# Attention on one core: lows of q and k formed by VectorE from the bank, exponentials joined for four sums a head group

## The chip, the cores and the metric

One core of one Trainium2 chip runs the whole program in one launch. The metric is the device time of one execution in microseconds (us); the median of several executions stands for a kernel. The engines are TensorE (PE; its weight loads are PEld), VectorE (DVE), ScalarE (ACT), GpSimd (POOL) and SyncE (SP, which issues DMAs).

## The reference

The reference is one transformer block with conditioning, on x of 8 x 1024 x 512, 16 heads of 32, hidden width 2048:

```python
mod = silu(condition) @ Wada + bada
sh_a, sc_a, gt_a, sh_m, sc_m, gt_m = split(mod, 6, axis=1)
xm = layernorm(x, g1, be1) * (1 + sc_a) + sh_a
q, k, v = heads(xm @ Wqkv)
attn = softmax(where(causal, q @ k.T * 32 ** -0.5, -inf))
x = x + gt_a * ((attn @ v) @ Wproj + bproj)
xm = layernorm(x, g2, be2) * (1 + sc_m) + sh_m
x = x + gt_m * (gelu(xm @ W1 + b1) @ W2 + b2)
```

All of it is float32. Products are formed in fp32r, whose operands carry fewer bits, so an operand that needs more is kept as a high (rounded) and a low (what is left), and a product is the sum of three: high by high, high by low, low by high.

## The kernel before

**Stages.** Rows of x are taken in 16 blocks of 512 (`ia`). A block gives 12 items: items 0 to 7 are q and k of a head group (four heads) each, items 8 to 11 are v. The first three blocks are made alone, at the start. Then come 16 bodies (`u`), each with the attention of two head groups; bodies 0 to 12 (`with_a`) also make the items of block `u + 3`, and bodies 0 to 11 (`with_ln`) the layer norm, the turning and the modulation of block `u + 4`. The MLP of 32 blocks of 256 rows follows.

**Steps and slots.** A body has 40 steps, 20 to a head group; I write the steps of the first group as 0 to 19 and of the second as 20 to 39. A step is one chunk of scores: 128 keys by 256 queries (128 in chunks 7, 13, 17 and 19) of four heads. PE forms them in two halves (`scores`, L847, into `psT`), ACT takes the exponentials (`exps`, L1117, into the ring `e`), and two steps make a slot, for which PE forms the products with v one slot later (`values`, L885). Slots 3, 6, 8 and 9 hold chunks on the diagonal; POOL masks these (`mask`, L1675), and `values` waits for the semaphore `masked`.

**Sums of exponentials.** POOL adds the chunks of a slot and of the other slots of its group into a buffer of `es` (`half_add`, L1688, for the first chunk of a slot that isn't the first of its group; `add`, L1705, for the second; `add`, L1712, for the first slot of a group). PE then sums a buffer over the keys with products by ones into `psO`: `added_sums` (L858, 256 queries) for a group that ends in a slot off the diagonal, at steps 9, 15 and 19 (29, 35, 39); `diagonal_sums` (L902 and L907, 128 queries each) for slots 3, 6, 8 and 9. Before the change a group of heads has seven groups of slots (`SUM_GROUPS`): 0 to 2, 3, 4 and 5, 6, 7, 8, 9. Both functions wait for `added`.

**Items in a body.** `A_SHARES` says how many of an item's 12 products (L793 for q and k, L797 for v) stand in each step. An item whose first share is in an odd step starts behind that step's `values` (`late`); the others stand behind the step's scores. All items of a body use one PSUM bank (`psA`, bank 1), so an item waits until the one before is out of it. ACT copies the bank to `qk_hl` (`a_copy`, L1107, the full value in the place of the low); DVE makes the high from it (`a_high`, L1363, a maximum of the copy with itself that rounds); POOL subtracts (`a_low`, L1666); SP stores both. `formed` sets the lags of these steps. PE waits for `a_copied` alone. The turned rows of the next block (`a_turn`, L765, steps 23, 29, 33 and 35) use the same bank.

**VectorE's own order.** Maxima of scores are reduced from `psS` (`max_item`, L1375 adds the mask, L1379 reduces) at steps 1, 3, 5, 7, 9, 11, 15, 17 and 19 of each group; PE forms the next piece only when `psS` is read. `max_join` (L1386) stands at step 12, statistics (L1314) at 8, 10, 12 and 14, the aggregate and `veps` (L1321, L1323) at 15, `normalise` (L1330) at 17 to 20. POOL makes `rstd` (L1659) at step 15 and waits for `veps`.

Of the kernel before, what the change touches and what calls it, by code (L numbers as in the profile page):

```python
# [5 lines left out]
ALU = mybir.AluOpType  # L6
# [3 lines left out]
F32R = mybir.dt.float32r  # L10
# [14 lines left out]
SLOTS = NCH // 2  # L25
# [8 lines left out]
AHEAD = 3  # L34
A_TURNS = 4

A_NQK, A_NV = 8, 4
A_ITEMS = A_NQK + A_NV
A_MM = 12
A_SHARES = ((6, 0, 6), (2, 8, 2), (6, 0, 6), (1, 5, 1, 5), (2, 8, 2), (5, 1, 5, 1)) * 2  # L40
A_STORE_LAG = 2

LATE_END, HIGH_LATE, LOW_LATE, STORE_LATE = 5, 2, 3, 4


Q, K = 0, 1
HIGH = (1, 0)
LOW = (0, 1)
QK_RING = 4
V_RING = 4  # L50

TURN_AT, TURN_AFTER = (23, 29, 33, 35), (7, 9, 10, 11)
# [95 lines left out]
DIAG_SLOTS = [i for i in range(SLOTS) if 2 * i in DIAG]  # L148
OTHER_SLOTS = [i for i in range(SLOTS) if i not in DIAG_SLOTS]

SUM_GROUPS = {True: [(0, 1, 2), (3,), (4, 5)] + [(i,) for i in range(6, SLOTS)], False: [(i,) for i in range(SLOTS)]}

HALF_ADDED = [i for g in SUM_GROUPS[True] for i in g[1:]]
HALF_ADDS = len(HALF_ADDED)
# [45 lines left out]
def build(nc, x, cond, Wqkv, Wproj, bproj, W1, b1, W2, b2, g1, be1, g2, be2, Wada, bada, out):  # L200
# [26 lines left out]
    with ExitStack() as keep:  # L227
        sems = {}

        def sem(name):  # L230
            if name not in sems:
                sems[name] = keep.enter_context(nc.semaphore(name))
            return sems[name]
# [116 lines left out]
        A_NLO = A_NQK  # L350
# [58 lines left out]
        def item_bank(n, alone):  # L409

            return n % 2 if alone and n <= TURN_AFTER_ALONE[0] else 1
# [13 lines left out]
        def _(sp):  # L425
# [30 lines left out]

            def a_store(ia, n):

                sp.wait_ge(sem("a_lo_done"), ia * A_NLO + n + 1)
                past(sp, "sp")  # L460
                sp.dma_start(qk_dram[n % 2, n // 2, :, :, bass.ds(ia * XB, XB)],
                             qk_hl[:, n % QK_RING]).then_inc(qk_stored[n % QK_RING], 16)
# [252 lines left out]
        def _(pe):  # L715
# [35 lines left out]
            def a_turn(ia, k, alone):  # L751

                bank = turn_bank(ia, k, alone)
                if k == 0:
                    pe.wait_ge(sem("xn_ready"), ia + 1)
                if not alone:
                    pe.wait_ge(sem("a_copied"), (ia - 1) * A_ITEMS + TURN_AFTER[k])
                elif ia > 0 and k == 0:
                    pe.wait_ge(sem("a_copied"), (ia - 1) * A_ITEMS + TURN_AFTER_ALONE[0])
                elif ia > 0:  # L760
                    pe.wait_ge(sem("a_modulated"), ia * A_TURNS + k)
                elif k >= 2:
                    pe.wait_ge(sem("a_modulated"), k - 1)
                for r in range(NXR):
                    mm = pe.transpose(psA[:, bank, r * P:(r + 1) * P], normalised(ia)[:, r, k * P:(k + 1) * P], ident[:])  # L765
                mm.then_inc(sem("a_turned"), 1)

            def a_item(ia, n, first, end, alone, turns):


                bank = item_bank(n, alone)
                if first == 0:
                    if alone and ia == 0 and n < 2:
                        pe.wait_ge(sem("a_modulated"), A_TURNS - 1 + n)
                    elif alone and n == 0:
                        pe.wait_ge(sem("a_modulated"), ia * A_TURNS + A_TURNS)
                    elif alone and n == 1:
                        pe.wait_ge(sem("a_copied"), ia * A_ITEMS)
                    elif alone and n <= TURN_AFTER_ALONE[0]:
                        pe.wait_ge(sem("a_copied"), ia * A_ITEMS + n - 1)  # L780
                    elif turns and n in TURN_AFTER:
                        pe.wait_ge(sem("a_modulated"), (ia + 1) * A_TURNS + TURN_AFTER.index(n) + 1)
                    else:
                        pe.wait_ge(sem("a_copied"), ia * A_ITEMS + n)
                for q in range(first, end):
                    k = q // 3
                    if n == 0 and q % 3 == 0:
                        pe.wait_ge(sem("xm_lo"), ia * KT + k + 1)
                    ends = dict(start=(q == 0), stop=(q == A_MM - 1), skip_group_check=True)
                    if n < A_NQK:  # L790
                        m = n % 2 * IPB + n // 2
                        a, w = ((xm_h, wqkv_h), (xm_l, wqkv_h), (xm_h, wqkv_l))[q % 3]
                        mm = pe.matmul(psA[:, bank, :], w[:, k, m * P:(m + 1) * P], a[:, k, :], **ends)  # L793
                    else:
                        m = n - A_NQK
                        a, w = ((xm_h, wqkv_h), (xm_h, wqkv_l), (xm_l, wqkv_h))[q % 3]
                        mm = pe.matmul(psA[:, bank, :], a[:, k, m * P:(m + 1) * P], w[:, k, 2 * D:3 * D], **ends)  # L797
                    if n == A_ITEMS - 1 and q % 3 == 2 and k < KT - 1:
                        mm.then_inc(sem("xm_freed"), 1)
                if end == A_MM and first < A_MM:  # L800
                    mm.then_inc(sem("a_formed"), 1)
# [268 lines left out]
        def _(act):  # L1070
# [26 lines left out]
            def a_copy(ia, n, alone):  # L1097

                if n < A_NQK:
                    wait(act, qk_stored[n % QK_RING], (ia * (A_NQK // QK_RING) + n // QK_RING) * 16)  # L1100
                    dst, src = qk_hl[:, n % QK_RING, LOW[n % 2]], psA[:, item_bank(n, alone), :]
                else:
                    m = n - A_NQK
                    wait(act, v_stored[m % V_RING], (ia * (A_NV // V_RING) + m // V_RING) * 16)
                    dst, src = vout[:, m % V_RING], psA[:, item_bank(n, alone), :]
                act.wait_ge(sem("a_formed"), ia * A_ITEMS + n + 1)
                act.activation(dst, src, ACT.Copy).then_inc(sem("a_copied"), 1)  # L1107
# [167 lines left out]
        def _(dve):  # L1275
# [79 lines left out]
                dve.wait_ge(sem("xm_hi"), ia * KT + k + 1)  # L1355
                dve.tensor_tensor(low, modulated(ia, k), high.bitcast(F32), ALU.subtract).then_inc(sem("xm_lo"), 1)

            def a_high(ia, n):

                if n < A_NQK:  # L1360
                    dve.wait_ge(sem("a_copied"), ia * A_ITEMS + n + 1)
                    full = qk_hl[:, n % QK_RING, LOW[n % 2]]
                    dve.tensor_tensor(qk_hl[:, n % QK_RING, HIGH[n % 2]].bitcast(F32R), full, full, ALU.max)\  # L1363
                       .then_inc(sem("qk_hi"), 1)

            def max_item(u, ahead, n, masks):

# [27 lines left out]
            def body(u, with_a, with_ln, after_a):  # L1395
                last = isinstance(u, int) and u == NU - 1
                for s in range(BODY_STEPS):
                    h, r = divmod(s, NCH)
                    if r == JOIN_AT and not (last and h == 1):
                        max_join(u, h + 1)  # L1400
                    if r == MAX_TURN_AT and not (last and h == 1):
                        max_row(u, h + 1)
                    if with_a and s == SPLIT_LAST_AT and not (isinstance(u, int) and u == 0):
                        a_split(u + AHEAD, KT - 1)
                    if with_ln and s in SPLIT_AT:
                        a_split(u + AHEAD + 1, SPLIT_AT[s])
                    if r in MAX_AT:
                        d, n = MAX_AT[r]
                        if not (last and h + d >= 2):
                            max_item(u, h + d, n, with_a)  # L1410
                    item = formed(u, s, 1, HIGH_LATE, with_a, after_a)
                    if item:
                        a_high(*item)
                    if with_ln and s in LN_STATS_AT:
                        ln_stats(u + AHEAD + 1, LN_STATS_AT.index(s))
                    if with_ln and s == LN_AGGR_AT:
                        ln_aggregate(u + AHEAD + 1)
                    if with_ln and s in LN_NORM_AT:
                        normalise(u + AHEAD + 1, LN_NORM_AT.index(s))
# [215 lines left out]
        def _(pool):  # L1635
# [89 lines left out]
            def body(u, with_a, with_ln, after_a, pieces):  # L1725
                for s in range(BODY_STEPS):
                    mask(u, s)
                    if s % 2 == 0:
                        half_add(u, s // 2, with_a)
                    else:  # L1730
                        add(u, s // 2, with_a)
                    item = formed(u, s, 1, LOW_LATE, with_a, after_a)
                    if item:
                        a_low(*item)
                    if with_ln and s == LN_AGGR_AT:
                        a_rstd(u + AHEAD + 1)
                    if isinstance(u, int) and u == NU - 1 and s == FIRST_RSTD_AT:
                        rstd_2(0)
                    for part in range(2):
                        q = PIECE_AT.get(s - PIECE_LOW_LAG - 2 * part)  # L1740
                        if q is not None and q < pieces:
                            piece_low(u, q, part)
# [76 lines left out]
```

## Time and profile before

| what | value |
|---|---|
| median of 3 executions | 3148.65 us (3148.61 to 3149.07) |
| the profiled execution | 3149.18 us, span 3147.5 us |
| granted TensorE clock, mean of the span | 0.999 |
| busy: PE, DVE, POOL, ACT | 98%, 78%, 54%, 45% |
| chain that ended last: PE, DVE | 90%, 5% |
| stage of items alone | 0 to about 149 us |
| 16 bodies | about 149 to 1547 us |
| MLP | about 1547 us to the end |

Busy shares are means over stages with different limits. A PE row's end is modelled, so consecutive PE rows overlap: what a group of products costs is read from its start to the start of the next group.

### The profile page before, as it was taken

The numbers are of one execution on the slowest core, as the hardware profiler recorded it, in microseconds if no ns is written. First come the engines' busy times: TensorE is split into PE (matmuls) and PEld (weight loads), VectorE is DVE, ScalarE is ACT, GpSimd is POOL, SyncE is SP. The second block draws the span as 40 slices with busy tenths as digits, with TensorE's granted clock in tenths as the row PEclk, the third lists the DMA queues.
The fourth block names the chain that finished last, engine by engine and source line by source line (L and its number), as shares of the span: only waits on it lengthen the run. The fifth ranks groups of instructions, "written<-read, shape, count | busy, mean of one in ns | idle before, by whom it ended". The sixth has DMA issues, their size and how long they took to land.

```text
span 3147.5 us, 64741 instructions
## 1 busy us (share of the span) xinstructions
PE 3099.2 (98%) x22888; PEld 2417.4 (77%) x22888; DVE 2451.6 (78%) x2975; ACT 1429.7 (45%) x2876; POOL 1704.9 (54%) x1385
## 2 busy tenths in 40 slices
PE   8999999999999999999899999999999999999999
PEld 5677777777777777766688888888888888888888
DVE  5688887787888778766787878878787787878874
ACT  4355555555555555566543333333333333333333
POOL 3388888888888888888742323232322322323232
PEclk9999999999999999999999999999999999999999
DMA  7666566666656666676713222221222313222120
GB/s 251 211 191 193 170 193 183 177 188 184 194 174 187 183 177 187 181 192 178 180 41 81 57 63 68 52 80 46 74 57 63 79 41 80 57 63 67 53 67 14
DMA packets 304625, 391.81 MB, mean 124 GB/s; under 512 B 24296, under 2 KB 206088, under 8 KB 304448
## 3 DMA queue, kind: packets, MB, share of 16 engines
q1 hardware_dynamic: 292336, 371.86, 41.7%
q10 hardware_dynamic: 12112, 17.42, 1.6%
q8 instruction: 132, 2.16, 0.3%
q14 instruction: 45, 0.37, 0.0%
HBM read 270.66 MB, written 118.00 MB: 123 GB/s over the span
## 4 chain that ended last, share of the span: by engine, by line
PE 90%; DVE 5%; issue 2%; DMA 1%; ACT 1%; POOL 1%; SPq 0%; DVEq 0%; ACTq 0%; POOLq 0%
PE psY L1025 22%; PE psH L1013 14%; PE psA L793 9%; PE psT L847 9%; PE psH L1016 7%; PE psA L885 7%; PE psA L797 6%; PE psP L922 6%; PE psS L816 4%; DVE mx L1379 2%; PE psA L858 2%; PE psA L765 1%; DVE psS L1375 1%; PE psA L907 1%; PE psA L902 1%
## 5 line engine op out<-in xcount | busy, mean ns | idle before, releaser
L1654 POOL TENSOR_TENSOR h_l<-h_full,h_h 128x256 fp32r<-128x256 f32 x512 | 451.2, 881 | 1099.5 <-ACT h_h L1255 1099.5
L1117 ACT ACTIVATE e<-psT 128x512 f32<-128x512 f32 (+1 forms) x1202 | 605.6, 555 | 377.0 <-PE psT L847 373.6
L1379 DVE TENSOR_REDUCE mx<-psS 128x4 f32<-128x2048 f32 (+3 forms) x384 | 665.9, 1755 | 118.6 <-PE psS L816 80.5
L1252 ACT ACTIVATE h_full<-h_full,b1c 128x256 f32<-128x256 f32 x512 | 260.4, 509 | 995.1 <-DVE h_full L1555 995.1
L1013 PE MATMUL psH<-a_l,w1p_h 128*128 128x512 f32 x2048 | 547.7, 389 | 1.0 <-ACT o_sb L1125 0.8
L1555 DVE TENSOR_REDUCE h_full<-psH 128x256 f32<-128x512 f32 x512 | 346.8, 677 | 238.8 <-PE psH L1016 230.6
L1712 POOL TENSOR_TENSOR es<-e 128x512 f32<-128x512 f32 (+1 forms) x242 | 444.9, 1839 | 159.5 <-ACT e L1117 75.6
L1013 PEld LDWEIGHTS psH<-a_l,w1p_h 128*128 128x128 f32 x2048 | 384.1, 188 | 83.1 <-ACT o_sb L1125 1.0
L847 PEld LDWEIGHTS psT<-qst,kst 97*128 97x128 f32 x2404 | 349.1, 189 | 113.7 <-issue 70.2
L847 PE MATMUL psT<-qst,kst 97*128 97x256 f32 (+1 forms) x2404 | 410.4, 290 | 3.4 <-ACT e L1117 1.7
L1025 PE MATMUL psY<-w_h,h_h 128*128 128x512 f32 x1024 | 404.2, 395 | 0.8 <-POOL h_l L1654 0.8
L1025 PE MATMUL psY<-w_l,h_h 128*128 128x512 f32 x1024 | 403.9, 394 | 0.0
L1025 PE MATMUL psY<-w_h,h_l 128*128 128x512 f32 x1024 | 398.4, 389 | 0.0
L1016 PEld LDWEIGHTS psH<-a_l,w1p_l 128*128 128x128 f32 x2048 | 313.1, 189 | 39.9
L1016 PE MATMUL psH<-a_l,w1p_l 128*128 128x256 f32 x2048 | 325.4, 282 | 0.0
L885 PE MATMUL psA<-e,vst 128*32 128x256 f32 (+1 forms) x5120 | 313.3, 362 | 0.3 <-POOL e L1675 0.2
L885 PEld LDWEIGHTS psA<-e,vst 128*32 128x32 f32 x5120 | 144.0, 109 | 114.0 <-issue 34.9
L1531 DVE STREAM_TRANSPOSE a_full<-xc 32x256 f32<-32x256 f32 x512 | 223.4, 436 | 9.4
L1467 DVE RECIPROCAL sums_in<-sums_in 128x256 f32<-128x256 f32 x128 | 222.7, 1743 | 7.9 <-DMA sums_in<-sums 7.8
L1666 POOL TENSOR_TENSOR qk_hl<-qk_hl 128x512 fp32r<-128x512 f32 x128 | 166.9, 1306 | 112.9 <-ACT qk_hl L1210 64.6
L1025 PEld LDWEIGHTS psY<-w_h,h_l 128*128 128x128 f32 x1024 | 192.5, 188 | 43.6
L1255 ACT ACTIVATE h_h<-h_full 128x256 fp32r<-128x256 f32 x512 | 214.2, 418 | 16.3
(118 smaller groups left out, 4927.5 us busy)
## 6 DMA issues: line engine op xcount, KB each, us to landing
qk_split<-qk_hl SPq DMA_DIRECT2D x128, 512.0 KB, 3.6
kst<-qk_split SPq DMA_DIRECT2D x128, 256.0 KB, 3.9
qst<-qk_split SPq DMA_DIRECT2D x128, 256.0 KB, 4.1
xin<-in_x_dram SPq DMA_DIRECT2D x64, 256.0 KB, 3.6
values<-vout ACTq DMA_DIRECT2D x64, 256.0 KB, 2.4
kmx<-qk_split SPq DMA_DIRECT2D x32, 512.0 KB, 4.7
qmx<-qk_split SPq DMA_DIRECT2D x32, 512.0 KB, 5.8
kst<-qk_split SPq DMA_DIRECT2D x128, 128.0 KB, 3.9
```

The costliest lines, as they stand in the source:

```text
L793: mm = pe.matmul(psA[:, bank, :], w[:, k, m * P:(m + 1) * P], a[:, k, :], **ends)
L847: mm = pe.matmul(bank[:, d, 0:w], kst[0:97, hd, key_cols(kt, h)], qst[0:97, q0 // HALF, hd, q0 % HALF:q0 % HALF + w], start=True, stop=Tru ...
L885: mm = pe.matmul(psO[HD * hd:HD * (hd + 1), c:c + w], vst[:, h, kt, HD * hd:HD * (hd + 1)], e[:, (2 * t + d) % ERING, hd, 0:w], start=(kt ...
L1013: pe.matmul(psH[:, m % 4].rearrange("p (s r) -> p s r", s=2), w1_h[:, k, cols], a_hl[par][:, :, k, :], start=(k == 0), stop=(k == KT - 1), ...
L1016: mm = pe.matmul(psH[:, m % 4, 0:RA], w1_l[:, k, cols], a_h[par][:, k, :], start=False, stop=(k == KT - 1), skip_group_check=True)
L1025: mm = pe.matmul(psY[:, r, :], a[:, m % 4, r * P:(r + 1) * P], w[:, w2_at(m), :], start=(m == 0 and n == 0), stop=(m == FT - 1 and n == 2) ...
L1117: act.activation(e[:, s % ERING, 2 * hp:2 * hp + 2, 0:w], score_bank(s, hp, with_a)[:, :, 0:w], ACT.Exp, scale=SCALE).then_inc(sem("exp_do ...
L1252: act.activation(h_full[:, m % 4, :], h_full[:, m % 4, :], ACT.Gelu, bias=b1c[:, m:m + 1])\
L1379: reduce = dve.tensor_reduce(mx[:, part, :, qt], psS[:, :, col:col + w], AX_X, ALU.max)
L1555: dve.tensor_reduce(h_full[:, m % 4, :], psH[:, m % 4].rearrange("p (s r) -> p r s", s=2), AX_X, ALU.add)\
L1654: return pool.tensor_tensor(dst, full, high.bitcast(F32), ALU.subtract)
L1712: pool.tensor_tensor(to, first, second, ALU.add).then_inc(sem("added"), 1)
```

## The change

In the bodies (the stage alone is as it was) ACT's copy of a q or k item is rounded to fp32r on its way out and goes to the place of the high. DVE's `a_low` subtracts that high from the full value in the PSUM bank and writes the low; `a_high` of DVE and `a_low` of POOL are gone there. The bank is free for the next item, or for the first turn, when `a_low` has read it, so PE and SP now wait for its semaphore `a_lo_body`. `a_low` stands one step behind the end of the item, ahead of that step's `max_item`, where `a_high` stood behind it. `SUM_GROUPS` has four groups: 0 to 3, 4 to 6, 7 and 8, 9. `A_SHARES` gives shares of (4, 8, 0) where (2, 8, 2) stood, and (6, 0, 6, 0) for (5, 1, 5, 1).

```diff
-A_SHARES = ((6, 0, 6), (2, 8, 2), (6, 0, 6), (1, 5, 1, 5), (2, 8, 2), (5, 1, 5, 1)) * 2
+A_SHARES = ((6, 0, 6), (4, 8, 0), (6, 0, 6), (1, 5, 1, 5), (4, 8, 0), (6, 0, 6, 0)) * 2
-LATE_END, HIGH_LATE, LOW_LATE, STORE_LATE = 5, 2, 3, 4
+LATE_END, STORE_LATE = 5, 4
-SUM_GROUPS = {True: [(0, 1, 2), (3,), (4, 5)] + [(i,) for i in range(6, SLOTS)], False: [(i,) for i in range(SLOTS)]}
+SUM_GROUPS = {True: [(0, 1, 2, 3), (4, 5, 6), (7, 8), (9,)], False: [(i,) for i in range(SLOTS)]}
@@ a_store (SP)
-                sp.wait_ge(sem("a_lo_done"), ia * A_NLO + n + 1)
+                if isinstance(ia, int) and ia < AHEAD:
+                    sp.wait_ge(sem("a_lo_done"), ia * A_NLO + n + 1)
+                else:
+                    sp.wait_ge(sem("a_lo_body"), (ia - AHEAD) * A_NLO + n + 1)
@@ a_turn (PE)
-                if not alone:
+                if not alone and TURN_AFTER[k] <= A_NQK:
+                    pe.wait_ge(sem("a_lo_body"), (ia - 1 - AHEAD) * A_NLO + TURN_AFTER[k])
+                elif not alone:
@@ a_item (PE)
+                    elif not alone and 0 < n <= A_NQK:
+                        pe.wait_ge(sem("a_lo_body"), (ia - AHEAD) * A_NLO + n)
@@ a_copy (ACT)
+                    if not alone:
+                        dst = qk_hl[:, n % QK_RING, HIGH[n % 2]].bitcast(F32R)
@@ DVE
-            def a_high(ia, n):
+            def a_low(ia, n):
...
-                    full = qk_hl[:, n % QK_RING, LOW[n % 2]]
-                    dve.tensor_tensor(qk_hl[:, n % QK_RING, HIGH[n % 2]].bitcast(F32R), full, full, ALU.max)\
-                       .then_inc(sem("qk_hi"), 1)
+                    dve.tensor_tensor(qk_hl[:, n % QK_RING, LOW[n % 2]].bitcast(F32R), psA[:, item_bank(n, False), :],
+                                      qk_hl[:, n % QK_RING, HIGH[n % 2]], ALU.subtract).then_inc(sem("a_lo_body"), 1)
@@ body (DVE), ahead of max_item
+                    item = ended(u, s - 1, with_a, after_a)
+                    if item:
+                        a_low(*item)
@@ body (DVE), behind max_item
-                    item = formed(u, s, 1, HIGH_LATE, with_a, after_a)
-                    if item:
-                        a_high(*item)
@@ body (POOL)
-                    item = formed(u, s, 1, LOW_LATE, with_a, after_a)
-                    if item:
-                        a_low(*item)
```

Three places show how the change moves instructions. The first is POOL at steps 15 to 19 of a body with layer norm, before (`e` are exponentials, `es` their sums, `qk_hl` an item):

```order
L1712 TENSOR_TENSOR es<-e 128x1024
L1659 TENSOR_TENSOR rstd<-veps,power 128x4
L1675 AFFINE_SELECT e<-e 128x4x128
L1666 TENSOR_TENSOR qk_hl<-qk_hl 128x512
L1675 AFFINE_SELECT e<-e 128x4x128
L1712 TENSOR_TENSOR es<-e 128x4x128
```

and with the change:

```order
L1720 TENSOR_TENSOR es<-e 128x1024
L1667 TENSOR_TENSOR rstd<-veps,power 128x4
L1683 AFFINE_SELECT e<-e 128x4x128
L1696 TENSOR_TENSOR es<-es,e 128x1024
L1683 AFFINE_SELECT e<-e 128x4x128
L1713 TENSOR_TENSOR es<-es,e 128x4x128
```

Between the two masks of slot 8 an add of 1024 elements a partition stands in the place of the item's subtraction of 512.

The second is DVE at steps 11 to 15 of such a body, before:

```order
L1379 TENSOR_REDUCE mx<-psS 128x4
L1386 TENSOR_TENSOR mxc<-mx 128x32
L1314 BN_STATS stats<-xin 128x6
L1363 TENSOR_TENSOR qk_hl<-qk_hl 128x512
L1393 CAST m_row<-psS 32x128
```

and with the change:

```order
L1387 TENSOR_REDUCE mx<-psS 128x4
L1394 TENSOR_TENSOR mxc<-mx 128x32
L1323 BN_STATS stats<-xin 128x6
L1371 TENSOR_TENSOR qk_hl<-psA,qk_hl 128x512
L1401 CAST m_row<-psS 32x128
```

The order is the same; the fourth row, which nobody but POOL waited for, is now the one that frees the bank for item 4, at step 13.

The third is PE at step 19, before:

```order
L847 MATMUL psT<-qst,kst 128x128 x4
L793 MATMUL psA<-xm_h,wqkv_l 128x512
L816 MATMUL psS<-kmx,qmx 128x512 x4
L858 MATMUL psA<-es,ones 32x256 x4
L885 MATMUL psA<-e,vst 32x256 x4
L885 MATMUL psA<-e,vst 32x128 x4
L902 MATMUL psA<-e,ones 32x128 x4
L907 MATMUL psA<-es,ones 32x128 x4
```

and with the change:

```order
L854 MATMUL psT<-qst,kst 128x128 x4
L823 MATMUL psS<-kmx,qmx 128x512 x4
L892 MATMUL psA<-e,vst 32x256 x4
L892 MATMUL psA<-e,vst 32x128 x4
L914 MATMUL psA<-es,ones 32x256 x4
```

The sums of a slot off the diagonal (L858) are gone, those of slot 8 are one quad of 256 queries that wait for both adds, and the item's single product has moved to step 18.

## Rows read from the trace of the kernel before

**Rows 1.** The page, section 1: busy time and share of each engine.

```profile
PE 3099.2 (98%) x22888; PEld 2417.4 (77%) x22888; DVE 2451.6 (78%) x2975; ACT 1429.7 (45%) x2876; POOL 1704.9 (54%) x1385
```

**Rows 2.** Windows of 100 us: length, then busy PE, PEld, DVE, ACT, POOL.

```profile
700.00:800.00 100.00, 99.39 (x1007) 71.23 (x1006) 82.15 (x75) 57.52 (x114) 82.28 (x54) 1.00 0.63 184
```

**Rows 3.** Timeline, PEld: step 3 in two consecutive bodies (start, duration).

```profile
705.21 0.30 PEld L816 LDWEIGHTS psS<-kmx,qmx 32*128 32x128 f32 x8 [0.20 <-DVE mx L1379]
...
797.27 0.30 PEld L816 LDWEIGHTS psS<-kmx,qmx 32*128 32x128 f32 x8 [0.20 <-DVE mx L1379]
```

**Rows 4.** Timeline, PE at step 9: sums, values, diagonal sums, then item 3.

```profile
718.90 0.64 PE L858 MATMUL psA<-es,ones 128*32 128x256 f32 x8
...
719.36 0.83 PE L885 MATMUL psA<-e,vst 128*32 128x256 f32 x16
...
720.01 0.40 PE L902 MATMUL psA<-e,ones 128*32 128x128 f32 x8
...
720.23 0.40 PE L907 MATMUL psA<-es,ones 128*32 128x128 f32 x8
...
720.56 0.50 PE L793 MATMUL psA<-xm_h,wqkv_h 128*128 128x512 f32 x1
```

**Rows 5.** Groups by form, 300 to 1500 us: POOL's full add (busy, mean ns).

```profile
L1688 POOL TENSOR_TENSOR es<-es,e 128x1024 f32<-128x1024 f32 x67 | 159.8, 2385 | 5.8 <-ACT e L1117 3.5
```

**Rows 6.** By source line, DVE: duration in ns, min/median/max, first and last start.

```profile
L1363 DVE TENSOR_TENSOR qk_hl<-qk_hl x104: 676/1016/2511, 156.6 to 1315.1; 128x512 fp32r<-128x512 f32 x104
L1375 DVE TENSOR_TENSOR psS<-psS,mask_q x135: 698/1217/1233, 92.2 to 1316.6; 128x1024 f32<-128x1024 f32 x81, 128x512 f32<-128x512 f32 x54
L1323 DVE TENSOR_SCALAR veps<-aggr x16: 169/1617/1636, 14.5 to 1196.2; 128x4 f32<-128x4 f32 x16
```

**Rows 7.** Timeline, steps 11 to 13: POOL, DVE, ACT's copy of item 3, PE's item 4.

```profile
725.42 2.39 POOL L1688 TENSOR_TENSOR es<-es,e 128x1024 f32<-128x1024 f32 x1
726.93 0.93 DVE L1386 TENSOR_TENSOR mxc<-mx 128x32 f32<-128x32 f32 x1
727.00 0.60 ACT L1107 ACTIVATE qk_hl<-psA 128x512 f32<-128x512 f32 x1 [0.29 <-PE psA L793]
727.78 0.68 DVE L1314 BATCH_NORM_STATS2 stats<-xin 128x6 f32<-128x512 f32 x1
728.23 0.50 PE L793 MATMUL psA<-xm_h,wqkv_h 128*128 128x512 f32 x1
728.39 2.44 DVE L1363 TENSOR_TENSOR qk_hl<-qk_hl 128x512 fp32r<-128x512 f32 x1
```

**Rows 8.** Timeline, steps 15 to 19: exponentials of step 15, POOL, `veps`, PE's sums.

```profile
732.14 0.59 ACT L1117 ACTIVATE e<-psT 128x512 f32<-128x512 f32 x1
734.65 2.39 POOL L1712 TENSOR_TENSOR es<-e 128x1024 f32<-128x1024 f32 x1
735.43 1.63 DVE L1323 TENSOR_SCALAR veps<-aggr 128x4 f32<-128x4 f32 x1
737.14 1.39 POOL L1659 TENSOR_TENSOR rstd<-veps,power 128x4 f32<-128x4 f32 x1
738.51 0.63 POOL L1675 TENSOR_SCALAR_AFFINE_SELECT e<-e 128x512 f32<-128x512 f32 x1
739.11 1.29 POOL L1666 TENSOR_TENSOR qk_hl<-qk_hl 128x512 fp32r<-128x512 f32 x1
741.43 1.28 POOL L1712 TENSOR_TENSOR es<-e 128x512 f32<-128x512 f32 x1 [0.26 <-POOL e L1675]
742.86 0.43 PE L907 MATMUL psA<-es,ones 128*32 128x128 f32 x8
```

**Rows 9.** Timeline, step 23: ACT's copy of item 6, PE's maxima, PE's first turn.

```profile
749.67 0.60 ACT L1107 ACTIVATE qk_hl<-psA 128x512 f32<-128x512 f32 x1 [0.44 <-PE psA L793]
750.04 0.51 PE L816 MATMUL psS<-kmx,qmx 32*128 32x256 f32 x8
750.48 0.66 PE L765 MATMUL psA<-ident,xin 128*128 128x128 f32 x4
```

## The prediction

> **What bounds the kernel now.** The page comes first: PE is busy for 98% of the span, no other engine for more than 78% [rows 1]. The change touches only the 13 bodies that make items, so I read the windows of that stage next: PE 99.4 us of 100, POOL and DVE 82.3 and 82.2 each [rows 2]. So PE's own work sets the time there, but two engines follow at four fifths, and both share the step order with PE. The same step of two consecutive bodies lies 92.06 us apart [rows 3]: that is my unit, and every term below is counted per body. The timeline of one body then tells what stands near PE's waits. Twelve bodies have the layer norm; one has not.
>
> **What it takes from PE.** Three sums of slots off the diagonal go in each head group. One costs 719.36 - 718.90 = 0.46 us, from its start to that of `values` [rows 4]. Six a body: -2.76 us. The joined slots 3, 6 and 8 had two quads of 128 queries, 0.22 us to the next start and 0.33 to the item's [rows 4]; now they have one quad of 256, which at the price of L858 is 0.46 and some 0.1 of the change to the next tile. 0.55 against 0.56: nothing. The number of items' products is the same; fewer and larger shares I set at 0. If all else stayed hidden, 26 head groups would give 26 x 3 x 0.46 = 36 us.
>
> **What it moves to and from POOL.** Eight subtractions of 1.29 us [rows 8] leave a body, and six full adds of 2.39 us come [rows 5]: +4.0 us, so 82 becomes about 89% of a body that PE would run in 89.3 us. On average that still fits. Locally it doesn't, see (b).
>
> **What it puts on PE's path.** Before, an item waited for ACT's copy alone. Now it waits for copy, then DVE. DVE's new subtraction isn't in this trace. Its bounds: the instruction that it replaces, two operands from SBUF, took 676 to 2511 ns, median 1016; the mask's add, one operand from a bank and one from SBUF, took 698 at 512 elements, and 1217 to at most 1233 at 1024, so without spread [rows 6]. I take 0.70, the row with the same kinds of operands, and keep 1.02 and 2.51 as the far end. A DVE instruction of 32 elements ended just when POOL's add did (see a). The Trainium skill (SBUF — State Buffer, "SBUF: two separate sides") has a rule that fits it: a DVE instruction with two SBUF inputs and a GpSimd instruction that reads SBUF shut each other out for the whole instruction. By it the 0.70 holds, since one input comes from a bank, and the sum is the one below; but the rule also speaks against the change, since more full adds on GpSimd hold the join and its like more often. Now the places, each against the timeline:
>
> (a) *Step 13, item 4.* PE starts it at 728.23 in the trace; the copy of item 3 ended at 727.60. DVE was then in the join (0.93 us for 32 elements, to 727.86, while POOL's add ended at 727.81) and in the statistics; it began `a_high` at 728.39, which held up nobody on PE [rows 7]. In the changed kernel PE gets there about 0.35 us earlier, 727.87: 0.46 gained at step 9, 0.1 lost there on `added`. DVE ends the reduction of step 11 at about 726.0, 0.9 earlier (no `a_high` ahead of it). But POOL's half add of slot 5, at 725.42 in the trace behind two subtractions [rows 7], now starts with its exponentials at about 722.5, the second add runs from 724.9 to 727.3 and holds the join till then. Join 727.3, statistics (0.60 to the next start) 727.9, low 728.6. PE waits 728.6 - 727.87 = 0.75 us.
>
> (b) *Steps 15 to 20, POOL.* In the trace PE waited for POOL's add of slot 8 already: it ended at 742.71, the sums began at 742.86, 0.29 later than the quad before them allows [rows 8, 4]. In the changed kernel the exponentials of step 15 end at about 733.8 instead of 732.73 (two products more in step 13, the wait of (a), and ACT's copy of item 4 now ahead of them). POOL: add of slot 7 from 733.97 to 736.35; `veps` isn't held by it any more and takes 0.17 [rows 6], so `rstd` runs from 736.6 to 738.0; mask 0.63, dependence 0.26, full add 2.38 in the place of the subtraction of 1.28, mask up to 0.8, 0.26, add 1.28: end at 743.55. PE's own way would reach these sums at about 742.0. With 0.15 of latency it goes on at 743.7, where before it did at 742.86, and then forms 256 queries. I make it a wait of 1.6 us more than before, and the first head group ends 1.0 us *later* than before although three of its sums are gone.
>
> (c) *Step 23, the first turn.* It begins 0.81 us after the start of the copy of item 6, right behind the maxima [rows 9]. Now copy (0.60), low (0.70) and two semaphores of 0.05 to 0.1 must end first: 1.43 us. PE waits 0.6.
>
> (d) Small ones at steps 7, 9 and 27 (the low ahead of the mask's add moves a reduction by up to 0.4) and less waiting at 11: +0.15 together. In the second head group POOL's slot 8 ends just as PE comes; nothing more there.
>
> **The sum.** A body with the norm: -2.76 + 0.75 + 1.6 + 0.6 + 0.15 = +0.3 us; twelve give +4. The body without norm has no `rstd` and no statistics: (a) falls to 0.2, (b) to 0.4, (c) is absent, so -2.0. Together +2 us on 3149.18 of the profiled execution, which lies 0.5 above the median of the runs: 3150.7, say 3151 us. So the forecast is no change that a measurement could tell; it tells about 0.2%, 6.3 us, from none. Its own range: each of the three waits may be off by 0.3 us a body, 12 x 0.5 = 6 us: 3144 to 3157.
>
> **Rivals.**
> *The waits don't form.* If POOL's add doesn't hold the join in (a), the low ends before 727.9, the exponentials of step 15 come 0.75 earlier and all of (b) with them: 12 x 0.75 = 9 us less, 3142. If the masked and joined adds of (b) also end in time, 12 x 2.35 = 28 us less: 3123; without any wait 3113. For it: the stalls of POOL on L858 go too, and DVE sheds 8 x (1.02 - 0.70) us a body at the medians. Against it: (b) follows from durations that hardly vary, and (c) is latency alone.
> *Slower: the low is locked out by POOL.* If DVE's subtraction behaves as the instruction that it replaces, 1.02 us at the median, both (a) and (c) grow by 0.32, and a full block of 1.8 us is possible at either. Two blocks of half that size are 2 x 0.9 x 12 = 22 us, the median 2 x 0.32 x 12 = 8: 3159 to 3173. It decides from a mean of 0.95 us on. Against it: the mask's add doesn't vary.
> *Slower: POOL becomes the bound in the second group as well.* Its slot 8 ends with no margin; 0.5 us there are 6 us, and delays carry over to the next body: 3157 to 3163.
> *The change doesn't do what it says.* The order shows that it does; no case of its own.
>
> **How the numbers follow.** Forecast (waits eat the gain) 0.44. The waits mostly don't form: 0.31. Slower by the low 0.13, by POOL 0.12, of which 0.01 lies within 0.2%. Cut at 6.3 us: faster 0.31, same 0.45, slower 0.24. The range reaches down to 3126, where (a) and most of (b) are gone, and up to 3163; what is left out is the case of next to no wait, 0.1, and that of a low blocked at its worst, 0.1.
>
> **What would show it.** Right: rows of L892 and L914 that start about 1 us late at step 19 and name POOL; a turn (L772) at step 23 and item 4 at step 13 that name DVE's low, L1371; a low of 0.70 without spread; a body of 92.3 us. Wrong: a body of 90 to 91 us with no such waits (the first rival), a spread of L1371 up to 2.5 us (the second), PE waits for POOL at step 39 (the third).

## The result, and the profile after

Median of 6 executions: 3161.52 us (3160.38 to 3162.35), against 3148.77 (3148.28 to 3149.07, 6 executions) for the kernel before, run in turn on the same chip. The ratio is 1.0040, with a 95% interval of 1.0028 to 1.0052. The change makes the kernel 12.7 us slower. That lies in the range (3126 to 3163), but the forecast was no change, 3151 us and at most 3157 by its own bounds, and the measurement tells 12.7 us from none.

The page, section 1, of the changed kernel [as rows 1], and the window of 100 us in the stage of the bodies [as rows 2]; the last three numbers of the window's row are the granted clock, the DMA share and GB/s:

```profile
PE 3069.3 (97%) x21640; PEld 2392.1 (76%) x21640; DVE 2418.3 (77%) x2975; ACT 1430.5 (45%) x2876; POOL 1747.8 (55%) x1359
```

```profile
700.00:800.00 100.00, 95.27 (x883) 67.53 (x872) 79.29 (x73) 56.19 (x111) 86.32 (x54) 1.00 0.63 184
```

PE has 1248 matmuls less and is busy 30 us less, and yet the span grew from 3147.5 to 3159.9: in the window it is idle for 4.7 us of 100, where before it was 0.6. POOL went from 82.3 to 86.3. Step 3 of two consecutive bodies [as rows 3]:

```profile
806.31 0.30 PEld L823 LDWEIGHTS psS<-kmx,qmx 32*128 32x128 f32 x8 [0.48 <-DVE mx L1387]
...
899.58 0.30 PEld L823 LDWEIGHTS psS<-kmx,qmx 32*128 32x128 f32 x8 [0.49 <-DVE mx L1387]
```

The period is 93.27 us, 1.21 more than before. From step 3 of body 0 to step 3 of body 12 the twelve bodies with the layer norm took 14.3 us more; the body without it took 85.28 us for 87.11, 1.8 less. The spans differ by 12.4. The timeline of PE in one body shows all its new waits (the bracket is the idle time and its releaser):

```profile
829.73 0.50 PE L800 MATMUL psA<-xm_h,wqkv_h 128*128 128x512 f32 x1 [0.76 <-DVE qk_hl L1371]
...
842.75 0.86 PE L892 MATMUL psA<-e,vst 128*32 128x256 f32 x16 [0.51 <-POOL e L1683]
...
844.19 0.64 PE L914 MATMUL psA<-es,ones 128*32 128x256 f32 x8 [0.58 <-POOL es L1713]
...
852.69 0.63 PE L770 MATMUL psA<-ident,xin 128*128 128x128 f32 x4 [0.59 <-DVE qk_hl L1371]
...
891.56 0.64 PE L914 MATMUL psA<-es,ones 128*32 128x256 f32 x8 [0.65 <-POOL es L1713]
...
894.99 0.56 PE L823 MATMUL psS<-kmx,qmx 32*128 32x128 f32 x8 [0.27 <-DVE mx L1387]
...
899.58 0.51 PE L823 MATMUL psS<-kmx,qmx 32*128 32x256 f32 x8 [0.28 <-DVE mx L1387]
```

In order: step 13 (a), step 19 twice (b), step 23 (c), and then three that the prediction's sum did not have: step 39, and steps 1 and 3 of the next body. A wait of 0.35 for ACT's `vout` at step 33 is left out; it was there before, as long and as often (4.2 us in 12). The same summed over the execution (total us, times, longest):

```profile
PE psA L914 <- POOL es L1713: 14.6, 24, 0.7
PE psS L823 <- DVE mx L1387: 11.0, 34, 1.2
PE psA L800 <- DVE qk_hl L1371: 9.5, 13, 0.9
PE psA L770 <- DVE qk_hl L1371: 7.2, 12, 0.6
...
PE psA L892 <- POOL e L1683: 6.4, 13, 0.5
```

Of these only L823 had a counterpart before, with 5.2 us in 16 waits. The new subtraction, by source line [as rows 6], in ns:

```profile
L1371 DVE TENSOR_TENSOR qk_hl<-psA,qk_hl x104: 660/691/693, 152.7 to 1322.0; 128x512 fp32r<-128x512 f32 x104
```

It hardly varies, where the instruction that it replaces went up to 2511.

What happens around step 39, DVE and POOL:

```profile
885.26 1.15 POOL L1683 TENSOR_SCALAR_AFFINE_SELECT e<-e 128x512 f32<-128x512 f32 x1 [0.57 <-ACT e L1126]
...
886.57 2.40 POOL L1696 TENSOR_TENSOR es<-es,e 128x1024 f32<-128x1024 f32 x1 [0.16 <-POOL e L1683]
...
888.49 0.76 DVE L1363 CAST xm_h<-xin 128x512 fp32r<-128x512 f32 x1
...
888.92 0.82 POOL L1683 TENSOR_SCALAR_AFFINE_SELECT e<-e 128x512 f32<-128x512 f32 x1
...
889.91 1.51 POOL L1713 TENSOR_TENSOR es<-es,e 128x512 f32<-128x512 f32 x1 [0.16 <-POOL e L1683]
890.21 1.49 DVE L1363 CAST xm_h<-xin 128x512 fp32r<-128x512 f32 x1
...
892.65 2.28 DVE L1387 TENSOR_REDUCE mx<-psS 128x4 f32<-128x2048 f32 x1
```

POOL's last add of slot 8 ends at 891.42; PE stood idle from 890.91 to 891.56. In the trace of before the same place had room:

```profile
783.83 1.77 POOL L1675 TENSOR_SCALAR_AFFINE_SELECT e<-e 128x512 f32<-128x512 f32 x2 [1.11 <-ACT e L1117]
785.86 1.28 POOL L1712 TENSOR_TENSOR es<-e 128x512 f32<-128x512 f32 x1 [0.26 <-POOL e L1675]
...
790.11 0.40 PE L907 MATMUL psA<-es,ones 128*32 128x128 f32 x8
```

There the add ended at 787.14, 2.97 us before PE came. POOL's chain from the first mask to the last add has grown from 3.31 us to 6.16, and PE would come 5.65 us after that mask's start where it came 6.28: so POOL is 0.51 late, and PE goes on 0.14 after it.

While these masks and adds run, DVE's splits of the next block take longer: a cast 0.76 and 1.49, where in the trace of before the two took 0.42 and 0.86. The reduction of step 39 starts 3.0 us after the start of its products (889.62), before 1.7; PE's maxima at step 1 wait for it, and those of step 3 for the next.

### The profile page after: what moved, and what is told of

It reads as the page before. It is cut to its first block, busy times and chain, and to the rows that moved or that the text cites. A ratio compares the mean times of both kernels' runs of the same rounds, so it can differ in the third digit from the quotient of the medians.

```text
span 3159.9 us, 62131 instructions
## 1 busy us (share of the span) xinstructions
PE 3069.3 (97%) x21640; PEld 2392.1 (76%) x21640; DVE 2418.3 (77%) x2975; ACT 1430.5 (45%) x2876; POOL 1747.8 (55%) x1359
## 4 chain that ended last, share of the span: by engine, by line
PE 80%; DVE 9%; issue 5%; POOL 2%; ACT 2%; DMA 1%; ACTq 0%; DVEq 0%; SPq 0%; POOLq 0%
PE psY L1032 22%; PE psH L1020 14%; PE psA L800 8%; PE psH L1023 7%; PE psT L854 6%; PE psP L929 6%; PE psA L892 5%; PE psA L804 5%; DVE mx L1387 5%; PE psS L823 3%; PE psA L770 1%; DVE psS L1383 1%; DVE xm_h L1363 1%; POOL es L1720 1%; PE psA L914 1%
## 5 line engine op out<-in xcount | busy, mean ns | idle before, releaser
L1720 POOL TENSOR_TENSOR es<-e 128x1024 f32<-128x1024 f32 (+1 forms) x164 | 338.8, 2067 | 142.7 <-ACT e L1126 128.9
L1696 POOL TENSOR_TENSOR es<-es,e 128x1024 f32<-128x1024 f32 x156 | 372.1, 2385 | 43.6 <-ACT e L1126 29.0
L892 PE MATMUL psA<-e,vst 128*32 128x256 f32 (+1 forms) x5120 | 314.8, 363 | 6.4 <-POOL e L1683 6.4
L1713 POOL TENSOR_TENSOR es<-es,e 128x1024 f32<-128x1024 f32 x156 | 289.4, 1855 | 20.2 <-POOL e L1683 10.8
L892 PEld LDWEIGHTS psA<-e,vst 128*32 128x32 f32 x5120 | 136.9, 109 | 123.8 <-issue 58.6
```

The source lines that it names most:

```text
L892: mm = pe.matmul(psO[HD * hd:HD * (hd + 1), c:c + w], vst[:, h, kt, HD * hd:HD * (hd + 1)], e[:, (2 * t + d) % ERING, hd, 0:w], start=(kt ...
L1696: pool.tensor_tensor(es[:, place], es[:, place], e[:, 2 * t % ERING], ALU.add)\
L1713: pool.tensor_tensor(to, to, second, ALU.add).then_inc(sem("added"), 1)
L1720: pool.tensor_tensor(to, first, second, ALU.add).then_inc(sem("added"), 1)
```

## The experiments

Eleven kernels ran, in three batches, each in turn with the kernel before (3149.5, 3149.1 and 3148.7 us); the third batch, of the last three kernels, on another chip than the first two. The question of the first four: which of the three parts costs what, and are they separate? The period is that of the turn's rows in the timeline (L770, or L765 before), around 300 to 650 us.

| kernel | median us | ratio, 95% interval | period us |
|---|---|---|---|
| before | 3149 | | 92.08 |
| the change | 3161.5 | 1.0028 to 1.0052 | 93.27 |
| shares alone | 3189.3 | 1.0108 to 1.0141 | |
| four sums alone | 3268.3 | 1.0356 to 1.0390 | |
| low from the bank alone | 3287.4 | 1.0411 to 1.0446 | |
| low and shares, seven sums | 3160.7 | 1.0023 to 1.0048 | 93.01 |
| the change, join at 13 | 3153.7 | 1.0005 to 1.0025 | 92.60 |
| low, shares, join at 13, seven sums | 3152.8 | 1.0002 to 1.0022 | 92.34 |
| the change, five sums | 3140.5 | 0.9965 to 0.9985 | 91.31 |
| **five sums, join at 13** | **3133.3** | 0.9932 to 0.9968 | 90.66 |
| before, with five sums | 3232.2 | 1.0240 to 1.0274 | |
| six sums, join at 13 | 3146.5 | 0.9983 to 1.0002 | 91.57 |
| five sums, join at 13, turn behind values | 3132.2 | 0.9927 to 0.9960 | 90.44 |

### Shares alone

Kernel before, with

```diff
-A_SHARES = ((6, 0, 6), (2, 8, 2), (6, 0, 6), (1, 5, 1, 5), (2, 8, 2), (5, 1, 5, 1)) * 2
+A_SHARES = ((6, 0, 6), (4, 8, 0), (6, 0, 6), (1, 5, 1, 5), (4, 8, 0), (6, 0, 6, 0)) * 2
```

> Only the shares of the items' products are changed (4, 8, 0 and 6, 0, 6, 0); q's and k's lows and the sums are as before. My theory (the loss comes from waits for the low, for joined sums and for VectorE behind GpSimd) gives no work and no wait here: within 3 us of before, body 92.1 +- 0.2 us. The rival that the shares themselves cost, because the exponentials of steps 5, 15 and 24 start two products (0.45 us) later: 0.3 us or more a body, 3152 to 3158.

3189.3 us: the expectation was wrong. An item that ends a step earlier brings DVE's maximum for its high a step forward, to where POOL's two adds of a joined slot run. Timeline of this run, POOL and DVE at steps 7 to 9, and PE's maxima at 9:

```profile
733.28 2.38 POOL L1705 TENSOR_TENSOR es<-es,e 128x1024 f32<-128x1024 f32 x1
...
733.55 2.66 DVE L1363 TENSOR_TENSOR qk_hl<-qk_hl 128x512 fp32r<-128x512 f32 x1
736.13 0.69 DVE L1375 TENSOR_TENSOR psS<-psS,mask_q 128x512 f32<-128x512 f32 x1
...
739.20 0.56 PE L816 MATMUL psS<-kmx,qmx 32*128 32x128 f32 x8 [1.22 <-DVE mx L1379]
```

The 0.7 us instruction takes 2.66, the mask's add and the reduction behind it are late, and PE waits 1.22 for `psS`. Over the execution these waits make nearly all of the 39.8 us lost, since before they came to 5.2:

```profile
PE psS L816 <- DVE mx L1379: 44.3, 43, 1.5
```

So the spread of rows 6, which cost nothing before, was a matter of place.

### Four sums alone

```diff
-SUM_GROUPS = {True: [(0, 1, 2), (3,), (4, 5)] + [(i,) for i in range(6, SLOTS)], ...
+SUM_GROUPS = {True: [(0, 1, 2, 3), (4, 5, 6), (7, 8), (9,)], ...
```

> Only the sums are joined; GpSimd keeps its subtractions. TensorE has 2.8 us a body less to do, GpSimd 14.3 us more (75.7 + 14.3 = 90.0 busy). Theory: GpSimd in its order becomes the bound of the body, with 1 to 3 us of dependences on top: body 91 to 94 us, 3140 to 3175, PE's waits name GpSimd's adds at slots 3, 6 and 8. Rival (GpSimd hides it): body 89.3 us, 3113.

3268.3, far above the expected. POOL, with its eight subtractions kept, is busy 815 us of the 900 from 200 to 1100, and PE waits for it:

```profile
PE psA L885 <- POOL e L1675: 64.0, 48, 2.9
PE psA L907 <- POOL es L1705: 33.8, 64, 0.6
```

98 us of waits less 36 us of sums taken from PE would be 62, and it came to 119: most of the rest went with PE's clock, by the estimate of the last section. The sum of waits for `psS` also went up, from 5.2 to 10.5 us.

### Low from the bank alone

The whole change but `A_SHARES` and `SUM_GROUPS`.

> Only the low is moved to VectorE; shares and sums are as before. Theory: item 4 at step 13 and the first turn at step 23 wait for the low, 0.5 to 0.8 and 0.6 us a body with the norm, and the 0.3 us wait for GpSimd at step 19 goes: +0.8 to +1.1 a body, 3158 to 3163; no PE wait on GpSimd. Rival (the low is harmless and the loss is all in the joined sums): 3146 to 3150.

3287.4, again far above. With the old shares an item that ends in step 5, 15, 19 or 25 leaves the next one, a step on, waiting for a low that stands behind a reduction on DVE. PE at step 16 of this run, and the waits summed (with 7.2 us of the turn's, as in the change, 103 in all):

```profile
708.67 0.49 PE L800 MATMUL psA<-xm_h,wqkv_h 128*128 128x512 f32 x1 [1.50 <-DVE qk_hl L1371]
```

```profile
PE psA L800 <- DVE qk_hl L1371: 68.6, 51, 2.1
PE psA L804 <- DVE qk_hl L1371: 26.9, 13, 2.1
```

So each of the three parts by itself makes the kernel slower, by 40, 119 and 138 us, and together they cost 13. The new shares are there for the low, and the low on DVE for the sums. None of the three can be priced alone.

### Low and shares, with the seven groups of before

> The changed kernel with the sums of before (low on VectorE, new shares). Theory: as with the low alone plus little from the shares, 3157 to 3165, so that the joined sums give in all about nothing (their 33 us of products go into waits for GpSimd and VectorE). Rival (the joined sums are what costs): 3148, 13 below the changed kernel.

3160.7, as expected. Its waits are two, and both are of those that the prediction priced:

```profile
PE psA L800 <- DVE qk_hl L1371: 8.9, 12, 0.9
PE psA L770 <- DVE qk_hl L1371: 7.1, 12, 0.6
```

0.74 and 0.6 us a body: (a) and (c). The waits of steps 19, 39, 1 and 3 aren't there. So the joined sums, which take 2.76 us a body from PE, bring those waits with them, and of the 2.76 us nothing is left: the body is 93.01 us without the joins and 93.27 with them.

### The join of the maxima behind the low (step 13)

```diff
-                    if r == JOIN_AT and not (last and h == 1):
-                        max_join(u, h + 1)
...
                     item = ended(u, s - 1, with_a, after_a)
                     if item:
                         a_low(*item)
+                    if r == JOIN_AT + 1 and not (last and h == 1):
+                        max_join(u, h + 1)
```

with the third statistics at step 13 as well (`LN_STATS_AT` 8, 10, 13, 14).

> The changed kernel, with VectorE's join of the maxima and the third statistics moved from step 12 to step 13, behind the low of item 3 (the step 12 ahead of the low is then empty). Theory (the join, held by GpSimd's add, keeps the low late, and by it the exponentials of step 15 and GpSimd's chain): PE's wait at step 13 for L1371 (0.76 us, 12 times) goes, and GpSimd's end at step 19 comes up to 0.7 us earlier: 0.8 to 1.4 us a body, 3145 to 3152 us. Rival (the join only moves to where the maxima's turn at step 14 waits for it): PE waits for L1394 at step 14 and the time stays at 3158 to 3164. Second rival (GpSimd's adds alone set step 19): only the 0.76 goes, or less, 3152 to 3158.

3153.7: 7.8 us of the change's 12.7 are gone (the theory's sum, 10 to 17, was too high; its second rival's figure fits). DVE around step 13 in this run:

```profile
545.56 0.69 DVE L1371 TENSOR_TENSOR qk_hl<-psA,qk_hl 128x512 fp32r<-128x512 f32 x1 [1.20 <-ACT qk_hl L1116]
546.17 0.18 DVE L1394 TENSOR_TENSOR mxc<-mx 128x32 f32<-128x32 f32 x1
```

The wait for L1371 at L800 (9.5 us) is no longer in the list. But the two rows of waits for POOL (L914 and L892) are word for word those of the change. So (a) and (b) are two causes. When the exponentials of step 15 come earlier, POOL's chain and PE come to step 19 earlier alike: POOL's last add of slot 8 ends 37.07 us after the products of step 3, where in the change it is 37.73.

> The same move of the join, with the seven groups of sums of the kernel before (so: lows from the bank, new shares, old sums). The run with these sums and without the move gave 3160.72 and had two waits on PE, 12 times each: 0.74 us for the low at step 13, 0.6 for the turn at step 23. Theory: the first goes, 9 us, 3150 to 3153. Rival: the wait moves to the maxima's turn, 3158 to 3162.

3152.8, as expected: with the seven sums the same move gives 8.0 us (93.01 to 92.34 a body).

### Slots 7 and 8 as groups of their own

```diff
-SUM_GROUPS = {True: [(0, 1, 2, 3), (4, 5, 6), (7, 8), (9,)], ...
+SUM_GROUPS = {True: [(0, 1, 2, 3), (4, 5, 6), (7,), (8,), (9,)], ...
```

> The changed kernel, but slots 7 and 8 are groups of their own again (five groups of sums). It gives back one sum of 0.46 us a head group, 0.92 a body, 12 us in all, and GpSimd's full add of 2.38 us between the masks of slot 8 is gone. Theory (POOL's slot 8 costs more than the sum it saves): the waits at steps 19 (0.51 + 0.58) and 39 (0.65) go, 1.7 us a body, and with them the waits for maxima at steps 1 and 3 if these come from the same lateness (0.55): net gain 0.8 to 1.4 us a body, 3145 to 3152. Rival (the waits only uncover something else of the same lateness, such as the exponentials): 3160 to 3170.

3140.5, 8.6 below the kernel before, and better than expected. PE has two sums a body more to form, 0.92 us, and yet the body becomes 1.96 us *shorter*. The rows of the waits for the low (9.5 and 7.2 us) are those of the change; what else is left of its waits:

```profile
PE psS L823 <- DVE mx L1387: 4.4, 10, 1.2
```

Both POOL lines are gone, and L823 went from 11.0 us in 34 waits to 4.4 in 10. At step 39 DVE is back to what it did before the change:

```profile
874.75 0.86 DVE L1363 CAST xm_h<-xin 128x512 fp32r<-128x512 f32 x1
...
876.25 2.29 DVE L1387 TENSOR_REDUCE mx<-psS 128x4 f32<-128x2048 f32 x1
```

The reduction starts 1.4 us after its products (874.81) instead of 3.0. That settles steps 1 and 3: they hung on POOL's work of slot 8 at step 39, by way of DVE's splits. The join of 7 and 8 thus cost 0.92 + 1.96 = 2.9 us a body for 0.92 gained. The waits that the trace names are 0.51 + 0.58 + 0.65 + 0.27 + 0.28 = 2.3 of it; 0.6 isn't named by any row.

> Both: the join moved to step 13, and slots 7 and 8 apart. If the two causes are separate, the gains add up: 3136 to 3144 us, below the kernel before (3148.8), with the turn's wait of 0.6 us at step 23 left. If they are one (the low of step 13 is what makes GpSimd late at step 19): the same as the better of the two, 3145 to 3152.

3133.3 us, ratio 0.995 (0.9932 to 0.9968): the two gains add (93.27 - 0.67 - 1.96 = 90.64, measured 90.66), the time is a little below the 3136 to 3144 expected, and this version beats both kernels. PE is busy 98.85 of 100 us in the window of 700 to 800, POOL 83.91. One wait of the change is left, the turn's, with the row that it had (L770, 7.2 us in 12 waits).

### What the low is for, and what slot 6 is worth

Kernel before with the five groups:

> The kernel before (full copy, high on VectorE, low on GpSimd, its shares) with the five groups of sums of the run before this one: 0 to 3, 4 to 6, 7, 8, 9. Theory (the lows on GpSimd leave no room for joined slots 3 and 6; only with them gone do these joins pay): PE waits for GpSimd (L1675, L1705) at slots 3 and 6, 1.5 us each as in the run with four groups (3268), but not at slot 8: 3190 to 3235 us. Rival (the five groups pay whoever forms the lows, and four groups failed by slots 7 and 8 alone): 3149 - 24 = 3125 to 3135 us.

3232.2, as the theory said. POOL and PE at slot 6 of this run:

```profile
756.26 2.37 POOL L1705 TENSOR_TENSOR es<-es,e 128x1024 f32<-128x1024 f32 x1
...
758.59 0.64 POOL L1675 TENSOR_SCALAR_AFFINE_SELECT e<-e 128x512 f32<-128x512 f32 x1
...
759.39 2.38 POOL L1688 TENSOR_TENSOR es<-es,e 128x1024 f32<-128x1024 f32 x1 [0.16 <-POOL e L1675]
...
761.72 1.09 POOL L1675 TENSOR_SCALAR_AFFINE_SELECT e<-e 128x512 f32<-128x512 f32 x1
...
762.96 0.86 PE L885 MATMUL psA<-e,vst 128*32 128x256 f32 x16 [1.49 <-POOL e L1675]
```

An item's subtraction at 752.55 (1.29 us) stands ahead of the adds of slot 5, and from there POOL has next to no gap up to slot 6's second mask, for which `values` wait 1.49 us. With the lows on DVE the same five groups bring no wait for POOL at all. So the move of the low earned nothing by itself (with seven sums and the join at 13, where it costs least, the kernel takes 3152.8 against 3149.1); it made room for the joins of slots 3 and 6. This run has the old shares as well. The new ones go with the low on DVE, and what they would do here with the low on POOL was not run.

Five groups and the join at 13, but slot 6 alone (`(0, 1, 2, 3), (4, 5), (6,), (7,), (8,), (9,)`):

> The best kernel so far (3133.3: join of the maxima at step 13, groups 0 to 3, 4 to 6, 7, 8, 9) with slot 6 a group of its own. Theory (a joined slot that makes nobody wait is worth PE's sum in full): 26 sums of 0.46 us come back, 12 us: 3144 to 3147. Rival (GpSimd's load costs something even without a wait on PE, so that only a part of the sum is won): 3136 to 3141.

3146.5, as the theory said: 13.2 us more, 0.91 a body, against two sums of 0.46 by rows 4. Where the added POOL work makes nobody wait, the sum's price is won in full. The same table prices the join of slot 3, which is all that tells this kernel from the one with seven sums and the join at 13: 92.34 to 91.57, 0.77 of the 0.92; PE has no new wait, and what the other 0.15 are isn't shown.

### The first turn behind step 23's values

```diff
+A_SHARES = A_SHARES[:7] + ((0, 12, 0),) + A_SHARES[8:]
...
-                    if turn and piece:
+                    if turn and piece and s != TURN_AT[0]:
                         a_turn(u + AHEAD + 1, TURN_AT.index(s), False)
...
                         values(u, t - 1)
+                        if turn and s == TURN_AT[0]:
+                            a_turn(u + AHEAD + 1, 0, False)
```

> The best kernel so far with the first turn (L770) of step 23 behind that step's values, and item 7's products all in step 24 (0, 12, 0 in the place of 4, 8, 0). The turn waited 0.6 us, 12 times, for the low of item 6 while nothing else was offered to PE. Theory (values fill the wait; what then remains is ScalarE's modulation ahead of item 7, some 0.3 us): a gain of 0.2 to 0.5 us a body, 3127 to 3131. Rival (the modulation is late by all that the turn gave, or twelve products in one step keep the scores of step 25 from ScalarE): 3133 to 3140.

3132.2 (3128.7 to 3134.3), above the 3127 to 3131 of the theory, and it can't be told from 3133.3. The turn's wait is gone, and another stands for it:

```profile
PE psA L801 <- ACT xin L1106: 4.7, 12, 0.4
```

What remains of it is ScalarE's modulation, 0.39 us a body, as the theory said. The body is 0.2 us shorter, which would be 2.5 us; the medians show 1.1, less than these executions tell.

## Why the prediction was right in its parts and wrong in its sum

The time lies within the range, but not by the forecast. The forecast's own bounds were 3144 to 3157; 3161.5 is where the third rival stood, and the range was wide enough to hold it.

**What it takes from PE: right.** 0.46 us for a sum came out at 0.91 for two where nobody waits (slot 6), and at 0.77 for the two of slot 3.

**The new subtraction: right.** 0.70 was taken, without spread; it measured 0.66 to 0.69. The rule of the Trainium skill (SBUF — State Buffer, "SBUF: two separate sides") agrees with both halves of what the traces show: this instruction, with one input from a bank, was never held, while the maximum with two inputs from SBUF took 2.66 us beside POOL's adds in the run with the shares alone. The second rival (low locked out, 0.13) is out.

**(a): right, 0.76 for 0.75.** The cause is shown too: with the join behind the low the wait is gone.

**(b): right place, too large.** The exponentials of step 15 end at 834.90 in the new trace, 733.80 on the clock of the old one (101.10 less, by step 3): as predicted. But POOL's last add ends at 742.94 there, not at 743.55. `rstd` took 1.02 us instead of the 1.39 of rows 8, and the dependences behind the masks 0.16 instead of 0.26. PE waited 1.09 in all. From the maxima of step 15 to the scores of step 20 lie 11.01 us where there were 10.97; with two sums less (0.92) that is 0.96 more of waiting, not 1.6. Nor was (b) a consequence of (a): the first rival's "all of (b) with them" fell in the run with the join moved.

**(c): right, 0.59 for 0.6.**

**The failed step: "In the second head group POOL's slot 8 ends just as PE comes; nothing more there".** The maxima's products of step 3 to those of step 29 took 1.23 us more than before; (a) to (d) and three sums less make 1.72. From step 29 to the next step 3 the prediction has three sums less, -1.38; measured -0.02. So the first part was 0.5 too dear and the second 1.4 too cheap, and 0.9 a body is 11 us: the whole miss. A margin of nothing was booked as nothing. PE waited 0.65 us there, of which 0.51 are POOL's lateness. The trace of before had what such a walk needs: POOL had 2.97 us there, a full add with its dependence takes 2.55 of it and the sum that PE no longer forms in step 39 another 0.46. What came on top are 0.2 of longer masks, 0.23 of a longer last add and 0.14 until PE goes on. And DVE's casts for the next block took longer beside POOL, so that two maxima waited 0.55 more, in steps that the change doesn't touch. Of the 1.4 these waits are 1.2; the rest no row names. The third rival said this much (a wait for POOL at step 39, delays that carry over, 3157 to 3163), and its time and its mark are what came. It was given 0.12, since 0.5 us was its guess rather than a walk through steps 35 to 40, as (b) had for 15 to 20.

**The body without norm: right,** -1.8 for -2.0.

## What to carry to other kernels

Where two engines meet with no margin, walk the timeline there in full and put the case where the second engine is late into the sum, not in a footnote: one joined slot cost 2.9 us for 0.92. Price joined work group by group: of three joined slots, each of them a price of 0.92 us a body, slot 6 earned 0.91 and slot 3 0.77, and slot 8 took back 1.96. And when parts of a change are each worse alone (here by 40, 119 and 138 us), undo them one at a time from the whole, not from the old kernel: only that led to the version at 3133.

## What the runs showed of the chip

A DVE instruction of 32 elements a partition (the join) took 1.34 to 1.49 us in all 22 instances of the changed kernel from 300 to 1300 us, at step 12, ahead of the low. Behind the low, with five groups and the join at 13, it took 0.18 to 0.28 in the first head group of these bodies and 1.33 to 1.36 in the second. What POOL runs beside it tells the two apart:

```profile
719.06 0.64 POOL L1683 TENSOR_SCALAR_AFFINE_SELECT e<-e 128x512 f32<-128x512 f32 x1
719.60 0.18 DVE L1394 TENSOR_TENSOR mxc<-mx 128x32 f32<-128x32 f32 x1
...
762.15 2.38 POOL L1713 TENSOR_TENSOR es<-es,e 128x1024 f32<-128x1024 f32 x1
763.22 1.36 DVE L1394 TENSOR_TENSOR mxc<-mx 128x32 f32<-128x32 f32 x1
```

In each of the long instances it ended some 0.05 us after POOL's add. `veps`, of 4 elements and with one input from SBUF, did the same: in the bodies with the layer norm it ended some 0.03 us after POOL's add. Before, it took 1.57 to 1.64 us there [rows 6]; in the changed kernel it starts closer to the end of the add and takes some 0.21, and 0.17 in the first body, where the add was over. The time of such an instruction is set by what POOL runs then, not by its size.

PE's clock gave way to waits. In the run of the kernel before with five groups, windows at slot 6 (length, busy PE, PEld, DVE, ACT, POOL, granted clock):

```profile
760.00:764.00 4.00, 2.33 (x31) 1.49 (x29) 4.00 (x4) 1.66 (x4) 3.84 (x3) 1.00 0.96 214
764.00:766.00 2.00, 1.61 (x10) 0.88 (x11) 1.97 (x3) 0.60 (x1) 2.00 (x3) 0.66 0.82 320
766.00:768.00 2.00, 2.00 (x9) 1.71 (x8) 2.00 (x2) 1.09 (x2) 1.80 (x1) 0.50 0.53 210
768.00:772.00 4.00, 4.00 (x36) 2.70 (x35) 3.13 (x3) 1.76 (x4) 3.57 (x2) 0.99 0.31 115
```

After waits of 1.49 and 0.58 us one behind the other the granted clock fell to 0.50, the lower level of 1.2 GHz, and came back when PE was busy again; two products of an item took

```profile
765.22 0.80 PE L793 MATMUL psA<-xm_h,wqkv_h 128*128 128x512 f32 x1
...
766.66 0.63 PE L793 MATMUL psA<-xm_l,wqkv_h 128*128 128x512 f32 x1
```

0.80 and 0.63 us instead of 0.50 [rows 4] and 0.39. Over 200 to 1100 us the mean clock of that run was 0.97. In the run with the low alone a single wait of 2.07 us, which ended at 320.40, went ahead of the same fall: the clock was 0.50 from 322 to 324. In the changed kernel, whose waits in the body shown are at most 0.76, it stayed at 1.00. So the longer waits cost more than themselves. How much, I can estimate from the mean clock of the profiled executions: it was 0.983 over the 3268 us of the run with four sums alone and 0.999 in the kernel before, and 0.016 of 3268 us is 52, or nearly all of the 57 that this run has beyond its waits and sums. In the run with the low alone it was 0.990, so some 30 us; with its 103 us of waits for the low that makes 133 of the 138 lost. No run separates the clock from the waits that go with it.
